# Four batches of a state-space and mixture-of-experts layer on one core: softplus in two groups, routing and scatters at earlier places of the loop, and the products with C shared out anew

## The chip, the cores and the metric

One core of a Trainium2 chip runs the whole layer in one launch. The number that counts is the device time of that launch in microseconds. The five engines (TensorE, VectorE, ScalarE, GpSimd, SyncE for transfers) each run their own list of instructions in order and meet only at semaphores.

## The reference, cut to what matters

x has 4 batches of 512 rows of 512. Three sublayers, each `x = x + f(layernorm(x))`:

```python
# 1 state-space mixer: 1024 channels d, 16 states n, 512 steps t
xz = in_proj @ x ; x, z = split(xz)
x = silu(depthwise_conv4(x)) ; dt, B, C = split(x_proj @ x)
delta = softplus(dt_proj @ dt + bias)            # [512, 1024]
h[t] = h[t-1] * exp(delta * A) + (delta * u) * B[t]   # for each d, n
y[t] = sum_n h[t] * C[t]
out = out_proj @ ((y + u * D) * silu(z))
# 2 an int8-quantised gated MLP, weights of each batch
# 3 mixture of experts: softmax router, top 2 of 16, plus 4 shared experts
```

## The kernel before

All is fp32 except the quantised integers (bf16). The 1024 channels lie as 8 blocks of 128 partitions, time along the free axis (512). The program of every engine is `phase1(b, b-1)` and `scan_stage(b, ...)` for b = 0 to 3, then `phase1(None, 3)` and a last stage without a scan.

**phase1(a, m)** interleaves two batches. For batch a: transposes of the normalised x (`head`), the projections `xi` with the convolution (`conv`, VectorE) and its silu, the small projections `bc_dt`, `dl` (input of the softplus, into bank 4 or 5), `z`, and the softplus. For batch m = a - 1: the last output of the mixer, the residual, and the quantised MLP (`Quant`: reduce, diag, scales, integers, transposed; `linear` on TensorE) in two layers. The order is written out by hand in each engine's phase1.

The softplus is relu(v) + ln(1 + e) - err/(1 + e) with e = exp(-|v|) and err the rounding error of 1 + e. ScalarE did it two blocks at a time: Abs, Exp, ReLU, plus one, Ln, and Exp(-Ln) for the reciprocal (L625 to L651), with a table load wherever the function changes. VectorE made the error term (L848), GpSimd added and subtracted (L484). z stood between the groups. Tiles: `pairs` and `work` serve as scratch; from the scan on they are the ring of products and `dBu`.

**scan_stage** is a loop over p = 0 to 135 on ScalarE, VectorE and TensorE, 128 scan units (block c // 16, state c % 16) and a tail; GpSimd loops over k, one pair of units each. Unit c: ScalarE writes exp(delta * A) into `R[c % 3]`, banks 4 to 6 (L666); GpSimd has made (delta * u) * B for two units, one *chunk* of 128 x 1024 (L521, four slots); VectorE runs the scan in place (L863) and one iteration later the product with C into `prod`, eight slots (L871); GpSimd adds the two products of a pair (L528, at k - 3), TensorE adds the sum into bank 7 by a product with the identity (L1336, at p = 2m + 5), and `gated` (L877, L880) closes each block of 16. From p = 113 TensorE also makes seven output products (`mixer_out`, L1486).

In the stages of b > 0 the experts of batch b - 1 stand between: 8 shared visits (p = 4 to 32, every fourth) and 23 routed ones (from p = 38, every third), each with gate and up products (L1383), tanh, two VectorE instructions and a down product (L1407). The router is cut in pieces on VectorE: `logits` (p = 5), `choice` in 7 steps from p = 10, `places` in 8 steps from p = 20, with `rank` on TensorE at p = 18. GpSimd then scatters the tokens to xs_dram (L541; k = 16 to 19, two transfers each, slot i and row tile t), SyncE reads them back in rows of 128 behind a wait for all scatters (`load_experts`), TensorE transposes them (`row_transposes`, L1367, first at p = 34). Results go to ys_dram, are gathered (L553, k = 60 to 63) and combined (L915, p = 130). The layernorm of the next batch's x runs inside too: statistics at p = 60, normalisation on VectorE (L824) at p = 66.

Of the kernel before, what the change touches and what calls it, by code (L numbers as in the profile page):

```python
# [92 lines left out]

def nsum_at(m):
    return 2 * m + (7 if m % (NS // 2) == 0 else 5)


LINKS = {"A": 1 + 2 * NBLK + NBLK, "LN": 8, "G": 40}
# [4 lines left out]
def build(nc, x, w_in, conv_w, xp_w, dt_w, dt_b, a_log, d_skip, out_w, gu_w, gu_wT, dn_w, dn_wT, gate_w,  # L103
          exp_w, out):
    with ExitStack() as ctx:
# [47 lines left out]
        rstd = sb("rstd", [P, TT])  # L153
        col = sb("col", [P, 9, 4])
# [50 lines left out]
        sp_inv = [late_pairs[:, i, :] for i in range(4)]  # L205
        sp_ln = [work[:, 2048 + i * T:2048 + (i + 1) * T] for i in range(4)]
        sp_w = [work[:, 4096 + i * T:4096 + (i + 1) * T] for i in range(4)]
# [13 lines left out]
        def width(v):  # L221
# [11 lines left out]
            "sp_abs sp_exp relu_ready sp_w_ready sp_ln_ready sp_inv_ready sp_err_ready sum_ready delta_ready "  # L233
            "du_ready dbu_ready da_ready scan_done prod_done pair_ready nsum_done y_done "
# [44 lines left out]
        def _(sp):  # L279
# [29 lines left out]
            def load_gate_up(b):  # L309
# [3 lines left out]
                sp.wait_ge(S["prod_done"], UNITS * b + UNITS - 12)  # L313
                sp.dma_start(guw, gu_w[b]).then_inc(S["xw_in"], 16)

            def load_mlp_down(b):

                sp.wait_ge(S["prod_done"], UNITS * b + UNITS - 4)
# [66 lines left out]
            def load_experts(be):  # L385
# [65 lines left out]
        def _(pool):  # L451
# [32 lines left out]
            def softplus(a, m):  # L484
                pool.wait_ge(S["sp_ln_ready"], NBLK * a + m + 1)
                nc.gpsimd.tensor_tensor(delta[:, m, :], delta[:, m, :], sp_ln[m % 4], ALU.add  # L486
                                        ).then_inc(S["sum_ready"], 1)
                pool.wait_ge(S["sum_ready"], NBLK * a + m + 1)
# [18 lines left out]
            def scan_stage(b, scan, experts):  # L507
# [8 lines left out]
                def chunk(k):  # L516
# [3 lines left out]
                    wait(pool, "scan_done", UNITS * b + 2 * (k - CHUNK_SLOTS + 1))  # L520
                    nc.gpsimd.tensor_tensor(  # L521
# [3 lines left out]
                def pair(m):  # L525
                    lo, hi = prod[2 * (m % PAIR_SLOTS)], prod[2 * (m % PAIR_SLOTS) + 1]
                    pool.wait_ge(S["prod_done"], UNITS * b + 2 * m + 2)
# [58 lines left out]
        def _(sc):  # L586
# [156 lines left out]
            def phase1(a, m):  # L743
                if a is not None:
                    for t in range(TT):
                        head(a, t)
# [873 lines left out]
```

## Time and profile before

| | us |
|---|---|
| median of 3 runs (2019.26 to 2023.7) | 2022.62 |
| the profiled execution | 2020.51 |
| its span | 2018.6 |
| scan stage of batch 0 | about 128 to 374 |
| scan stages of batches 1, 2, 3 | begin at 519, 980, 1441 |
| last stage, experts alone | from about 1822 |

A row of groups gives line, engine, operation, output <- inputs, shapes, count, then busy us, mean ns of one, idle us before them and what ended it. In the timeline a bracket holds the idle time before an instruction and its releaser. "(x16)" in the stage table is a count. One matrix product of fp32 shows as two MATMUL records.

### The profile page before, as it was taken

How to read it: one execution, taken by the hardware profiler on the slowest of the kernel's cores; microseconds unless marked ns; L12 is line 12 of the kernel's file. 1: busy time of each engine (PE TensorE's matmuls, PEld its weight loads, DVE VectorE, ACT ScalarE, POOL GpSimd, SP SyncE). 2: the span in 40 equal slices, each digit the busy share in tenths (PEclk: the TensorE clock that was granted, in tenths of full speed). 3: DMA queues.
4: the chain of work that ended last, by engine and by line, in shares of the span. 5: the costliest groups of instructions: out<-in, count | busy, mean ns of one | idle time of the engine just before them, and what ended most of it. 6: DMA issues, size and time to landing. Idle time of an engine off the chain costs nothing.

```text
span 2018.6 us, 18589 instructions
## 1 busy us (share of the span) xinstructions
PE 1413.2 (70%) x4944; PEld 790.7 (39%) x4952; DVE 1482.2 (73%) x2425; ACT 818.2 (41%) x1344; POOL 1135.8 (56%) x707
## 2 busy tenths in 40 slices
PE   7825546996574788897574777897575878648773
PEld 3301112443443454343442554343343554236562
DVE  3259999686695999686695999696596999673111
ACT  3753333257422454247522445147622554021121
POOL 0279999203867799302866889402767999300101
PEclk9965555997687999998687989998687999767996
DMA  3360000333124663522223664523213663402785
GB/s 99 126 234 0 0 0 5 136 121 110 68 74 144 200 202 127 182 88 97 100 77 130 205 192 140 189 73 114 103 66 120 216 218 125 182 0 79 247 296 171
DMA packets 99016, 255.23 MB, mean 126 GB/s; under 512 B 11488, under 2 KB 11616, under 8 KB 93792
## 3 DMA queue, kind: packets, MB, share of 16 engines
q1 hardware_dynamic: 91680, 233.08, 34.3%
q0 software_dynamic: 5120, 16.78, 2.4%
q10 hardware_dynamic: 2112, 4.19, 0.6%
q8 instruction: 40, 0.66, 0.1%
q14 instruction: 64, 0.52, 0.1%
HBM read 211.02 MB, written 42.99 MB: 126 GB/s over the span
## 4 chain that ended last, share of the span: by engine, by line
POOL 29%; PE 21%; DVE 19%; issue 15%; ACT 11%; DMA 4%; SPq 0%; POOLq 0%; DVEq 0%; ACTq 0%
POOL work L521 16%; DVE bank L863 6%; POOL work L528 5%; PE bank L1383 4%; POOL pairs L528 4%; PE bank L1296 3%; PE bank L1306 3%; DMA ew_up<-in_exp_w 2%; PE bank L1486 2%; DVE u L842 2%; DVE pairs L871 1%; DVE work L871 1%; POOL xs_dram L541 1%; PE bank L1343 1%; POOL du L513 1%
## 5 line engine op out<-in xcount | busy, mean ns | idle before, releaser
L863 DVE TENSOR_TENSOR_SCAN bank<-bank,work 128x512 f32<-128x512 f32 x512 | 624.1, 1220 | 30.2 <-POOL work L521 30.2
L666 ACT ACTIVATE bank<-delta,A_sb 128x512 f32<-128x512 f32 x512 | 353.5, 691 | 641.4 <-DVE pairs L871 325.1
L521 POOL TENSOR_TENSOR work<-du,BB 128x1024 f32<-128x1024 f32 x256 | 604.7, 2364 | 0.8
L1383 PEld LDWEIGHTS bank<-xT,ew_up 128*128 128x128 f32 x1472 | 200.2, 203 | 114.5 <-issue 90.8
L1383 PE MATMUL bank<-xT,ew_up 128*128 128x128 f32 x1472 | 208.8, 288 | 43.7 <-issue 24.0
L1336 PE MATMUL bank<-pairs,ident 128*128 128x512 f32 x256 | 160.8, 734 | 93.2 <-POOL pairs L528 66.7
L528 POOL TENSOR_TENSOR work<-work 128x512 f32<-128x512 f32 x128 | 162.7, 1272 | 62.0 <-DVE work L871 60.9
L1336 PE MATMUL bank<-work,ident 128*128 128x512 f32 x256 | 166.6, 744 | 42.4 <-POOL work L528 42.3
L528 POOL TENSOR_TENSOR pairs<-pairs 128x512 f32<-128x512 f32 x128 | 163.1, 1274 | 54.7 <-DVE pairs L871 53.3
L871 DVE TENSOR_TENSOR pairs<-bank,CB 128x512 f32<-128x512 f32 x256 | 172.2, 673 | 3.0 <-PE bank L1336 3.0
L871 DVE TENSOR_TENSOR work<-bank,CB 128x512 f32<-128x512 f32 x256 | 171.8, 673 | 0.0
L1407 PE MATMUL bank<-ew_dn,etm 128*128 128x512 f32 x184 | 108.3, 672 | 73.4 <-ACT xT L702 73.4
L1306 PE MATMUL bank<-xT,wst 128*128 128x512 f32 x256 | 124.0, 630 | 6.0 <-ACT zg L616 6.0
L1383 PE MATMUL bank<-x3T,ew_up 128*128 128x256 f32 x512 | 125.3, 401 | 0.5 <-DMA ew_up<-in_exp_w 0.5
L486 POOL TENSOR_TENSOR delta<-delta,work 128x512 f32<-128x512 f32 x32 | 52.9, 1652 | 128.2 <-ACT work L647 128.2
L1486 PE MATMUL bank<-wst,zg 128*128 128x512 f32 x256 | 120.1, 616 | 5.8 <-DVE zg L880 4.4
L471 POOL TENSOR_TENSOR col<-col,halfpow 128x4 f32<-128x4 f32 (+1 forms) x8 | 8.2, 1020 | 205.0 <-DVE col L981 205.0
L1296 PE MATMUL bank<-xT,wst 128*128 128x512 f32 x256 | 119.7, 615 | 2.7 <-ACT xT L594 2.7
L1367 PE MATMUL bank<-ident,hm 128*128 128x128 f32 x368 | 60.9, 292 | 81.1 <-DMA hm<-xs_dram 69.2
L887 DVE SCALAR_TENSOR_TENSOR etm<-etm,bank 128x128 f32<-128x128 f32 (+1 forms) x124 | 38.7, 312 | 104.1 <-ACT etm L691 99.3
L1336 PEld LDWEIGHTS bank<-pairs,ident 128*128 128x128 f32 x256 | 51.1, 225 | 162.8 <-POOL pairs L528 65.4
L1383 PEld LDWEIGHTS bank<-x3T,ew_up 128*128 128x128 f32 x512 | 103.1, 203 | 29.3 <-issue 12.9
(174 smaller groups left out, 2038.2 us busy)
## 6 DMA issues: line engine op xcount, KB each, us to landing
ew_up<-in_exp_w SPq DMA_DIRECT2D x124, 512.0 KB, 3.7
ew_dn<-in_exp_w SPq DMA_DIRECT2D x124, 256.0 KB, 4.1
hm<-xs_dram SPq DMA_DIRECT2D x92, 256.0 KB, 4.6
ys_dram<-xT SPq DMA_DIRECT2D x92, 256.0 KB, 4.3
wst<-in_w_in SPq DMA_DIRECT2D x64, 256.0 KB, 2.7
BB<-bc_dram SPq DMA_DIRECT2D x16, 1024.0 KB, 4.9
CB<-bc_dram SPq DMA_DIRECT2D x16, 1024.0 KB, 7.1
wst<-in_out_w SPq DMA_DIRECT2D x32, 256.0 KB, 3.6
```

The costliest lines, as they stand in the source:

```text
L521: nc.gpsimd.tensor_tensor(dBu[:, k % CHUNK_SLOTS, :, :], du[:, j % 2:j % 2 + 1, :].broadcast_to([P, 2, T]), BB[:, n0:n0 + 2, :], ALU.mult) ...
L528: nc.gpsimd.tensor_tensor(lo, lo, hi, ALU.add).then_inc(S["pair_ready"], 1)
L666: nc.scalar.activation(R[q % RING][:, :], delta[:, j, :], ACT.Exp, scale=A_sb[:, j, n:n + 1]).then_inc(S["da_ready"], 1)
L863: V.tensor_tensor_scan(R[q % RING][:, :], R[q % RING][:, :], dBu[:, c // 2 % CHUNK_SLOTS, c % 2, :], 0.0, ALU.mult, ALU.add).then_inc(S["s ...
L871: V.tensor_tensor(prod[c % (2 * PAIR_SLOTS)], R[q % RING][:, :], CB[:, n, :], ALU.mult).then_inc(S["prod_done"], 1)
L1296: ins = mm(ps[:, :], wst[:, slot, k * P:(k + 1) * P], xT[:, k, :], start=(k == 0), stop=(k == KD - 1))
L1306: ins = mm(bank[6 + m % 2][:, :], wst[:, slot, k * P:(k + 1) * P], xT[:, k, :], start=(k == 0), stop=(k == KD - 1))
L1336: mm(Y[:, :], ident[:], prod[2 * (m % PAIR_SLOTS)], start=(m % (NS // 2) == 0), stop=(m % (NS // 2) == NS // 2 - 1)).then_inc(S["nsum_done ...
L1367: ins = nc.tensor.transpose(rows_bank(r)[:, k * P:(k + 1) * P], xs[:, n % 2, k * P:(k + 1) * P], ident[:])
L1383: ins = mm(gu_bank(v)[:, part * n:(part + 1) * n], ew_up[:, q % UP_RING, part * D + k * P:part * D + (k + 1) * P], rhs, start=(k == 0), st ...
L1407: mm(down_ps[1][:, :], eT[:, v % 2, 0:P], ew_dn[:, q % DOWN_RING, :], start=True, stop=True).then_inc(S["down_done"], 1)
L1486: ins = mm(acc[t][:, :], zg[:, k, t * P:(t + 1) * P], wst[:, slot, :], start=(k == 0), stop=(k == NBLK - 1))
```

## The change

Softplus: two groups of four blocks. ScalarE keeps Abs, Exp and Ln; ReLU, plus one, the reciprocal and the last addition go to VectorE; GpSimd subtracts the error term. All z come after it or between its groups, and the scan's first decay waits for them. Routing: pieces at earlier p, two steps an iteration; the scatters at k = 11 and 12, four each, the gathers at 59 and 60. Products: unit c with c % 8 == 7 is scanned straight into `prod` and multiplied by C on GpSimd; pairs of odd m are no longer added by GpSimd, TensorE adds both products. The normalisation of the next x moves to ScalarE (p = 68 to 74), VectorE keeps the shift. The load of x stands behind three loads of rows.

```diff
-ROUTE_EXP_AT = 9
-ROUTE_PROB_AT = 10
-ROUTE_POS_AT = 20
-RANK_AT = 18
-RANK_VISIT = 4
-SCATTER_AT = 16
-GATHER_AT = 60
+ROUTE_EXP_AT = 6
+ROUTE_PROB_AT = 8
+RANK_AT = 14
+RANK_VISIT = 3
+ROUTE_POS_AT = 16
+SCATTER_AT = 11
+GATHER_AT = 59
+def on_pool(c):
+    return c % 8 == 7
+def dve_products(q):
+    return q - q // 8
...
 # SyncE, load_experts
-                if be + 2 < B:
-                    load_x(be + 2)
                 for j in range(ROUTED + 6):
+                    if j == 3 and be + 2 < B:
+                        load_x(be + 2)
...
 # GpSimd, softplus
-                nc.gpsimd.tensor_tensor(delta[:, m, :], delta[:, m, :], sp_ln[m % 4], ALU.add
...
-                nc.gpsimd.tensor_tensor(delta[:, m, :], delta[:, m, :], sp_w[m % 4], ALU.subtract
-                                        ).then_inc(S["delta_ready"], 1)
+                nc.gpsimd.tensor_tensor(delta[:, m, :], delta[:, m, :], sp_e[m % 4], ALU.subtract
+                                        ).then_inc(S["delta_less"], 1)
 # GpSimd, chunk and pair
+                    if k == 2:
+                        pool.wait_ge(S["delta_ready"], NBLK * (b + 1))
...
-                    nc.gpsimd.tensor_tensor(lo, lo, hi, ALU.add).then_inc(S["pair_ready"], 1)
+                    if m % 2 == 0:
+                        pool.wait_ge(S["prod_done"], dve_products(UNITS * b + 2 * m + 2))
+                        nc.gpsimd.tensor_tensor(lo, lo, hi, ALU.add).then_inc(S["pair_ready"], 1)
+                    elif on_pool(2 * m + 1):
+                        pool.wait_ge(S["scan_done"], UNITS * b + 2 * m + 2)
+                        nc.gpsimd.tensor_tensor(hi, hi, CB[:, (2 * m + 1) % NS, :], ALU.mult).then_inc(S["pool_prod"], 1)
 # ScalarE
+            def head_apply(a, t):
+                sc.wait_ge(S["x_in"], 16 * (a + 1))
+                sc.wait_ge(S["a_shift_ready"], a + 1)
+                nc.scalar.activation(xn[:, t, :], xn[:, t, :], ACT.Identity, scale=rstd[:, t:t + 1],
+                                     bias=shift[:, t:t + 1]).then_inc(S["a_xn_ready"], 1)
-            def softplus(a, pair):
-                ms = (2 * pair, 2 * pair + 1)
+            def softplus(a, group):
+                ms = range(4 * group, 4 * group + 4)
...                                                # Relu, Identity and Exp(-Ln) removed
 # VectorE
+            def relu(a, m):
+                ve.wait_ge(S["sp_abs"], NBLK * a + m + 1)
+                V.tensor_scalar(delta[:, m, :], bank[4 + m % 2][:, :], dtb[:, m:m + 1], 0.0, ALU.add, ALU.max
+                                ).then_inc(S["relu_ready"], 1)
+            def one_more(a, m):
...
+                V.tensor_scalar(sp_w[m % 4], sp_e[m % 4], 1.0, None, ALU.add).then_inc(S["sp_w_ready"], 1)
+            def lost(a, m):
...
+                link(V.scalar_tensor_tensor(out=sp_e[i], in0=sp_w[i], scalar=1.0, in1=sp_e[i],
+                                            op0=ALU.subtract, op1=ALU.subtract))
...
+                link(V.reciprocal(du[:, 1, :], sp_w[i]))
+                V.tensor_tensor(sp_e[i], sp_e[i], du[:, 1, :], ALU.mult).then_inc(S["sp_err_ready"], 1)
             def softplus(a, m):
                 ve.wait_ge(S["sp_ln_ready"], NBLK * a + m + 1)
+                ve.wait_ge(S["delta_less"], NBLK * a + m + 1)
+                V.tensor_tensor(delta[:, m, :], delta[:, m, :], sp_ln[m % 4], ALU.add).then_inc(S["delta_ready"], 1)
 # VectorE, order in phase1 (m's steps between): relu 0-3 | q1.reduce, diag, scales |
 #   one_more 0-3, lost 0-3 | q1.integers | softplus 0-3 | q1.transposed | relu 4-7 |
 #   second residual, statistics, norm | one_more 4-7, lost 4-7, softplus 4-7
 # TensorE, nsum
-                    mm(Y[:, :], ident[:], prod[2 * (m % PAIR_SLOTS)], ...)
+                    if m % 2 == 0:            # as before
...
+                    else:
+                        pe.wait_ge(S["prod_done"], dve_products(UNITS * b + 2 * m + 2))
+                        if on_pool(2 * m + 1):
+                            pe.wait_ge(S["pool_prod"], (UNITS * b + 2 * m + 2) // 8)
+                        mm(Y[:, :], ident[:], prod[2 * (m % PAIR_SLOTS)], start=False, stop=False)
+                        mm(Y[:, :], ident[:], prod[2 * (m % PAIR_SLOTS) + 1], start=False,
+                           stop=(m % (NS // 2) == NS // 2 - 1)).then_inc(S["nsum_done"], 1)
 # TensorE, order in phase1: ... bc_dt 6 | integers 0 | bc_dt 7 | linear 0 | dl 0, 1, z 0, dl 2, 3 |
 #   gated_rows | z 1 | diag_rows 1 | z 2 | scale_rows 1, integers 1 | dl 4, 5, z 3, dl 6, 7 | linear 1 | z 4-7
```

## Rows read from the trace of the kernel before

**Rows 1.** The page, engine busy time: us, share of the span, instructions
```profile
PE 1413.2 (70%) x4944; PEld 790.7 (39%) x4952; DVE 1482.2 (73%) x2425; ACT 818.2 (41%) x1344; POOL 1135.8 (56%) x707
```

**Rows 2.** Stage table: stretch, length, busy us (count), granted clock, DMA share, GB/s
```profile
125.00:379.00 254.00, 144.52 (x200) 44.10 (x200) 239.92 (x286) 87.78 (x128) 239.21 (x139) 0.59 0.12 44
379.00:520.00 141.00, 105.64 (x336) 49.63 (x336) 91.84 (x195) 83.80 (x127) 29.55 (x22) 0.87 0.29 105
520.00:840.00 320.00, 233.64 (x903) 146.67 (x904) 281.52 (x411) 119.67 (x210) 254.53 (x152) 0.86 0.45 147
...
720.00:760.00 40.00, 33.29 (x175) 23.06 (x176) 38.99 (x58) 21.65 (x40) 37.67 (x22) 0.96 0.70 222
```

**Rows 3.** Waits: VectorE, TensorE at 521:834; VectorE at 1442:1745 (total, times, longest)
```profile
DVE bank L877 <- PE bank L1336: 21.1, 1, 21.1
...
PE bank L1407 <- ACT xT L702: 24.4, 19, 3.5
...
DVE bank L877 <- PE bank L1336: 17.5, 1, 17.5
```

**Rows 4.** Timeline at 519:636: start, us, engine, line, operation [idle before, releaser]
```profile
519.43 9.26 POOL L521 TENSOR_TENSOR work<-du,BB 128x1024 f32<-128x1024 f32 x4
...
594.05 0.37 DVE L1242 CAST posi<-xT 128x8 uint32<-128x8 f32 x1
...
619.38 0.97 POOL L541 DMA_INDIRECT xs_dram<-xn,posi  x1 [2.34 <-issue]
...
628.41 1.11 PE L1367 MATMUL bank<-ident,hm 128*128 128x128 f32 x4 [22.70 <-DMA hm<-xs_dram]
...
634.35 0.76 DVE L877 SCALAR_TENSOR_TENSOR bank<-u,dsk,bank 128x512 f32<-128x512 f32 x1 [21.11 <-PE bank L1336]
```

**Rows 5.** Timeline, ends of the scan stages of batches 0 and 1
```profile
375.01 1.88 PE L1336 MATMUL bank<-work,ident 128*128 128x512 f32 x4
...
829.25 3.28 DVE L915 SCALAR_TENSOR_TENSOR ew_dn<-ew_dn,tw,x 128x512 f32<-128x512 f32 x3 [7.32 <-DMA ew_up<-ys_dram,posi]
```

**Rows 6.** Timeline, last stage: the places of the tokens, the rows read back
```profile
1863.93 0.17 DVE L1242 CAST posi<-xT 128x8 uint32<-128x8 f32 x1
...
1878.80 0.80 SPq L368 DMA_DIRECT2D hm<-xs_dram  x2
```

**Rows 7.** Groups by line; the last one at 521:834 alone
```profile
L863 DVE TENSOR_TENSOR_SCAN bank<-bank,work 128x512 f32<-128x512 f32 x512 | 624.1, 1220 | 30.2 <-POOL work L521 30.2
L521 POOL TENSOR_TENSOR work<-du,BB 128x1024 f32<-128x1024 f32 x256 | 604.7, 2364 | 0.8
...
L871 DVE TENSOR_TENSOR pairs<-bank,CB 128x512 f32<-128x512 f32 x256 | 172.2, 673 | 3.0 <-PE bank L1336 3.0
...
L528 POOL TENSOR_TENSOR pairs<-pairs 128x512 f32<-128x512 f32 x128 | 163.1, 1274 | 54.7 <-DVE pairs L871 53.3
...
L824 DVE TENSOR_SCALAR xn<-xn,mv,rstd 128x512 f32<-128x512 f32 x4 | 7.4, 1914 | 0.0
```

**Rows 8.** Timeline of batch 0's first phase: normalisation, one z
```profile
10.61 1.92 DVE L824 TENSOR_SCALAR xn<-xn,mv,rstd 128x512 f32<-128x512 f32 x4 [1.17 <-POOL rstd L471]
...
60.77 3.60 PE L1306 MATMUL bank<-xT,wst 128*128 128x512 f32 x8
```

**Rows 9.** Groups by line and shape: reciprocals, alone and second of two
```profile
L990 DVE RECIPROCAL col<-col 128x4 f32<-128x4 f32 x4 | 0.7, 178 | 0.1
...
L990 DVE RECIPROCAL col<-col 128x2 f32<-128x2 f32 x4 | 0.7, 166 | 0.1
...
L1175 DVE RECIPROCAL xT<-xT 128x4 f32<-128x4 f32 x4 | 0.6, 146 | 0.0
L1061 DVE RECIPROCAL col<-col 128x2 f32<-128x2 f32 x4 | 0.5, 134 | 0.0
```

**Rows 10.** Timeline of the phase before batch 1's scan
```profile
472.23 0.29 DVE L1023 TENSOR_SCALAR BB<-BB 128x256 bf16<-128x256 f32 x1 [5.14 <-ACT BB L731]
...
482.81 2.73 DVE L1038 SCALAR_TENSOR_TENSOR BB<-bank,rr,CB 128x512 f32<-128x512 f32 x4 [1.89 <-PE bank L1467]
```

More of the change, by code:

```diff
@@ L723, in scan_stage @@
                                 y_rows(r)
+                    if scan and b + 1 < B:
+                        for t in range(TT):
+                            if p == NORM_AT + 2 + 2 * t:
+                                head_apply(b + 1, t)
             def magic_rows(m, layer, side):
@@ L772, in phase1 @@
                     softplus(a, 0)
-                    z(a, 2)
-                    z(a, 3)
-                    softplus(a, 1)
+                    for i in range(3):
+                        z(a, i)
                 if m is not None:
@@ L780, in phase1 @@
                 if a is not None:
-                    z(a, 4)
-                    z(a, 5)
-                    softplus(a, 2)
-                if a is not None:
-                    z(a, 6)
-                    z(a, 7)
-                    softplus(a, 3)
+                    softplus(a, 1)
+                    for i in range(3, NBLK):
+                        z(a, i)
             for b in range(B):
@@ L923, in scan_stage @@
                         scan_unit(p)
-                    if scan and 1 <= p <= UNITS:
+                    if scan and 1 <= p <= UNITS and not on_pool(p - 1):
                         product(p - 1)
@@ L930, in scan_stage @@
                             logits(b - 1, link)
[L931 to L934 removed]
+                        for step in range(7):
+                            if p == ROUTE_PROB_AT + step // 2:
+                                choice(b - 1, link, step)
+                        for step in range(8):
+                            if p == ROUTE_POS_AT + step // 2:
+                                places(b - 1, link, step)
                         for v in range(VISITS):
@@ L1124, in phase1 @@
                     gated_rows(m)
+                if a is not None:
+                    for i in range(4):
+                        relu(a, i)
+                if m is not None:
                     q1.reduce()
                     q1.diag()
-                if a is not None:
-                    softplus(a, 0)
-                if m is not None:
                     q1.scales()
                 if a is not None:
-                    softplus(a, 1)
+                    for i in range(4):
+                        one_more(a, i)
+                    for i in range(4):
+                        lost(a, i)
                 if m is not None:
@@ L1135, in phase1 @@
                 if a is not None:
-                    softplus(a, 2)
+                    for i in range(4):
+                        softplus(a, i)
                 if m is not None:
@@ L1139, in phase1 @@
                 if a is not None:
-                    softplus(a, 3)
+                    for i in range(4, 8):
+                        relu(a, i)
                 if m is not None:
@@ L1146, in phase1 @@
                 if a is not None:
-                    softplus(a, 4)
-                    softplus(a, 5)
-                if a is not None:
-                    softplus(a, 6)
-                    softplus(a, 7)
+                    for i in range(4, 8):
+                        one_more(a, i)
+                    for i in range(4, 8):
+                        lost(a, i)
+                    for i in range(4, 8):
+                        softplus(a, i)
                     assert linkA[a].n == LINKS["A"], ("A", linkA[a].n)
```

136 lines of the change are left out of this document (65 added, 71 removed).

## The prediction

> **What bounds the kernel now.** I read the page's engine shares first [rows 1]: no engine is busy over 73% of the span, so the answer differs by stage. The table by stage [rows 2] splits it. The scan stage of batch 0 (125 to 379 us) has VectorE at 239.9 and GpSimd at 239.2 us of 254: both full. The scan stage of batch 1 with the experts of batch 0 (520 to 840) has VectorE at 281.5 of 320, GpSimd at 254.5, TensorE at 233.6. The phase between scans (379 to 520) has nobody full: a chain of waits over five engines. Then the waits by stage [rows 3]: in the stages of batches 1 and 2 VectorE stands once for 21.1 us at L877, in batch 3 for 17.5, always behind TensorE; and TensorE itself stands 22.7 us for the rows read back from xs_dram. The timeline [rows 4] tells the story: the places of the tokens are ready on VectorE at 594.05, the eight scatters end with the one at 619.38, the rows reach TensorE at 628.41. TensorE runs its instructions in order, so the sums of products behind that transposition stand still, and VectorE stops when it needs a finished block.
>
> **The routing and scatters sooner.** The places move from iteration 27 of the scan loop to iteration 19, the scatters from k = 16 to 19 to k = 11 and 12 of GpSimd's loop. An iteration costs 2.4 us there: the first chunk is done at 521.8, and VectorE begins its long wait, in iteration 37, at 634.35 - 21.11 = 613.2 [rows 4]. So the places come some 19 us sooner. The scatters then take 8 x 1.27 us plus the 2.34 us that the eighth waits [rows 4], and one chunk of 2.36 between: 15 us; landing and read-back take under 9 more (619.38 to 628.41, with a load of x ahead that now comes later). That is 24 us after iteration 19, and TensorE wants the rows at iteration 34, 14 iterations or 31 us later. The waits of 21.1, 21.1 and 17.5 us go: -59.7. Moved past the queues: on GpSimd four scatters (5.1 us) stand ahead of chunk 12 and four (7.6 us) ahead of chunk 13. VectorE holds four to six scan units ahead, about 9 us, against 17.5 us until chunk 13 is done: about 4 us of new starvation per stage, +12. On SyncE the load of x comes behind three loads of rows; its reader is at iteration 60, so that costs nothing. Gathers at k = 59 and 60 instead of 59+1 to 59+4: at the end of the stage VectorE waited 7.3 us for the last of them [rows 5]; that goes, but TensorE is late next (below), so 3 us: -9 in three stages. In the last stage, without a scan, the places come after one visit less: 1863.93 [rows 6] becomes about 1855.5 (TensorE ranks behind the third visit instead of the fourth, 5 us a visit, and VectorE no longer waits for a fourth and fifth expert). The rows are asked for at 1878.80 now [rows 6] and at 1870.3 then; TensorE's own visits hold it until 1876.7, and it began with the rows 2.6 us after the request, at 1881.4: -4.7 at least, -8.5 at most; I take -6.
>
> **Products.** One of eight products leaves VectorE. Of its 0.67 us [rows 7] 0.08 lie under the next instruction: 0.59, 16 times a stage. Sixteen scan units cost VectorE now 16 x 1.73 + 1.37 = 29.1 us, then 27.8. GpSimd's eight chunks, eight additions and one du cost 8 x 2.36 + 8 x 1.27 + 1.27 = 30.3 us [rows 7]; four additions fewer and two products more (a product taken at the price of an addition) make 27.8. The scan into SBUF instead of PSUM no row shows; I take the same 1.22, with 0.1 us either way, 6 us in all. In batch 0 the bound was GpSimd, 8 x 30.3 = 242.5; with both engines at 27.8 and a little jostling I take 28.2: -17. Behind it TensorE: 32 more sums a stage, each two records, and four records take 1.88 us at full clock with 0.15 of it the end of the last [rows 5]: 0.43 a record, 0.87 a sum. From iteration 113 it is full already, with 7 outputs of eight such records. The five more sums there end 4.3 us later, and that end starts the next phase. Batch 0: -17 + 4.3 = -12.7, say -12. In batches 1 to 3 VectorE is the bound: 16 x 0.59 = 9.4, and the normalisation of the next x, four instructions that take 7.4 us in these stages [rows 7] where four such took 1.92 with GpSimd idle [rows 8], goes to ScalarE (4 x 0.69, which waits for products 1 us at a time anyway): 7.4 less 0.2 for what stays. Together -16.6 in three stages, -49.8.
>
> TensorE in these stages: 320 - 233.6 = 86.4 us free, 27.8 more work and a stage 34 us shorter leave 24. The 24.4 us for ScalarE's copies [rows 3] I read as slack, since ScalarE comes to such a copy only behind the decays that follow VectorE's pace. But it is down to some 5% in the routed part, so I add 5 us a stage: +15.
>
> **The softplus in two groups of four.** What goes: ten of sixteen table loads a phase on ScalarE, the second exponential and one GpSimd addition. What comes, on VectorE, eight times a phase: ReLU 0.67, plus one 0.46 (four of its kind take 1.92, [rows 8]), a subtraction 0.70, a reciprocal, a product 0.62, a sum 0.61. No row shows a reciprocal of 512 elements. Small ones do [rows 9]: in the same place 4 elements take 178 ns and 2 take 166, and as the second of a pair 146 and 134: 12 ns for two elements both times, 6.2 ns each, so 178 + 508 x 6.2 = 3.35 us. From below the bound is 0.68 (the nearest full-size instruction, a reduction or product); from above 4.3 (the same rows with 2 ns of misreading on each side, 8 ns an element). I take 3.35, since two pairs agree. A group's four then take 4 x 4.7 = 18.8 us, and they are on the path.
> The Trainium skill (VectorE: DVE Perf Modes, the 8-slice pipeline) says the reciprocal iterates with a repeat count of 8 where simple operations give one result a cycle. By that rule at its 0.96 GHz (an estimate) it would be 4.27 us; the rows above stand at three quarters of it, and by it the sum would be 30 us longer.
>
> Phase of batch 1, step by step. Without z0 and z1 ahead of it the chain up to the first linear comes 1.5 us sooner, but the transposes of the gated rows wait behind dl2, dl3 and two ReLUs; the scales end near 463.9 instead of 465.8. Then plus one, 1.8, and the four, 18.8: VectorE reaches the integers at 484.5, where it now does at 472.23 [rows 10]. ScalarE, held by its Ln until then and by z2, is ready at 477. The first sums and the transposed integers, 3.8, the ReLUs of the second group behind dl6 and dl7, which stand behind z3: the second residual starts at 494.3 (482.81 now). Its 11.4 us to the end of the normalisation stay: 505.7. Plus one and four more: 526.4, GpSimd's subtraction and du 2.5: the first chunk at 528.9, against 519.43. +9.5 a phase, +28.5 in three. z7, which waits for ScalarE's Ln, ends at 521 and stays hidden. SyncE's weights of the output and the last two broadcasts wait for z4 to z7, until 520.8; they land by 535 and are wanted at 540.
> Phase of batch 0: the start is 4.5 us later, since ScalarE alternates between normalising and copying (four rounds of 2.6 us where VectorE took 1.92 in all and TensorE followed, [rows 8]); without z0 and z1 (3.60 us each, [rows 8]) the projections end 6.4 us sooner. Then 60 us to the first chunk, as now 58.7: -0.5.
>
> **Sum.** -0.5 - 12 + 28.5 - 59.7 + 12 - 9 - 49.8 + 15 - 6 = -81.5. The profiled execution took 2020.51 us (span 2018.6 and 1.9 around it), 0.1% below the median 2022.62. 2020.5 - 81.5 = 1939; 1940 on the scale of the median.
>
> **Rivals.**
> 1. The reciprocal is cheap, 0.7 us (for it: it is one instruction like the others; against: the slope of 12 ns in two pairs). Each group loses 10.6 us; the end is then held by z5 to z7, so the first scan comes 10 us before today's: 20 us less in four phases: 1862.
> 2. It costs 4.3 us: 32 x 0.95 = +30: 1970.
> 3. TensorE's slack is latency, not pace. Then most of the 27.8 us a stage is on the path (for it: TensorE is busy 33.3 of 40 us at 720 to 760, [rows 2]; against: no long wait of VectorE for a sum stands there). +17 in three stages: 1990.
> 4. Slower: TensorE's clock. It is granted 0.59 in batch 0's stage and 0.86 in batch 1's [rows 2], and one sum takes twice as long at the half level (1.2 GHz instead of 2.4). With the new work TensorE is the bound below (233.6 + 27.8) x 0.86 / 286 = 0.79, and the stage is as slow as before below 0.70. At 0.65 a stage takes 346 us, 26 more than now: 2020 - 12 + 28 - 6 + 78 = 2108. Against it: the long stall in which TensorE idles goes, and it has more to do.
>
> **Chances.** Forecast 0.58, rival 1 0.07, rival 2 0.13, rival 3 0.15, rival 4 0.07. The forecast's own spread (stall left over, bursts on GpSimd, scan into SBUF) is 20 us each way. 1906 to 1990 leaves out rivals 1 and 4 and a little more. Within 0.2% is what cannot be told from no change; only a mixture of 3 and 4 lands there, 0.02. Faster 0.91, slower 0.07.
>
> **What will show it.** Right: no wait of VectorE above 5 us at L877's counterpart inside stages 1 to 3; RECIPROCAL 128x512 near 3.35 us, 32 times; GpSimd busy some 20 us less a stage; the phases between scans near 150 us instead of 141; batch 0's scan stage near 242; TensorE above 90% busy in the routed part with a granted clock of 0.95. Wrong: a reciprocal off by 1 us moves the time by 30 us; VectorE idle for sums or chunks by more than 10 us a stage; a routed row still late.

## The result, and the profile after

| | before | after |
|---|---|---|
| median, us | 2019.26 (2014.76 to 2023.70, 5 runs) | 2012.45 (2006.61 to 2013.95, 5 runs) |
| ratio to before | | 0.9947, 95% interval 0.9931 to 0.9963 |
| span of the profiled execution, us | 2018.6 | 2011.6 |

The change gains half a per cent. The forecast was 1940, with 1906 to 1990 as its range, so it was wrong by far more than the measurement's uncertainty. Differences between kernels are given below in us as a difference of ratios times 2020.

The page of the changed kernel, engine busy time and the group of the new reciprocals (line, engine, operation, shapes, count, busy us, mean ns, idle before):

```profile
PE 1493.4 (74%) x5208; PEld 831.6 (41%) x5208; DVE 1595.8 (79%) x2477; ACT 728.3 (36%) x1232; POOL 1010.7 (50%) x611
...
L890 DVE RECIPROCAL du<-work 128x512 f32<-128x512 f32 x32 | 107.3, 3353 | 1.1
```

VectorE is busy for 114 us more than in [rows 1], though products were taken from it: the reciprocals alone are 107. The table of the changed kernel's stages, with the columns of [rows 2]:

```profile
135.00:374.00 239.00, 152.76 (x256) 56.02 (x257) 227.89 (x269) 88.87 (x131) 217.13 (x121) 0.78 0.18 69
374.00:530.00 156.00, 109.28 (x344) 50.34 (x344) 129.59 (x227) 60.46 (x96) 18.54 (x13) 0.86 0.23 80
530.00:832.00 302.00, 251.58 (x960) 153.88 (x961) 271.04 (x394) 119.73 (x212) 234.02 (x137) 0.90 0.50 164
```

The phase between two scans (second row) took 156 us where it took 141, and VectorE (third number) is busy for 130 us of it, where it was for 92. In the scan stage with experts (third row) VectorE has 10 us less to do, GpSimd 20 less, TensorE 18 more. VectorE's waits in that stage (waiter, releaser, us in total, times, longest):

```profile
DVE bank L908 <- POOL work L535: 14.9, 2, 8.5
DVE bank L922 <- PE bank L1398: 7.7, 4, 4.1
DVE pairs L916 <- PE bank L1391: 2.8, 1, 2.8
DVE xT L1214 <- PE bank L1405: 2.0, 1, 2.0
DVE work L908 <- PE bank L1398: 1.6, 1, 1.6
```

The wait of 21.1 us for TensorE [rows 3] is gone. In its place stand two waits for a chunk of GpSimd (14.9 us together) and nine shorter ones; the longest are shown. With the start of VectorE's work in each stage and the end of its last gated block as marks, the two traces divide as follows, in us:

| stretch | forecast | measured |
|---|---|---|
| phase of batch 0, to the first scan | -0.5 | 127.9+2.4 to 135.2+3.1: +8.0 |
| scan stage of batch 0 | -12 | 248.1 to 236.0: -12.1 |
| phases before batches 1 to 3 | +28.5 | 15.5, 13.3 and 14.2 longer: +43.0 |
| scan stages of batches 1 to 3: VectorE's busy time | -49.8 | -13.7, -13.7, -6.6: -34.0 |
| the same: its idle time (-59.7 +12 -9 +15) | -41.7 | 33.8 to 31.0, 33.7 to 31.8, 29.2 to 29.0: -4.9 |
| last stage | -6 | -7.0 |
| sum | -81.5 | -7.0 |

Three rows miss: idle time by 37 us, busy time by 16, the phases between the scans by 15; batch 0's phase adds 8. Below, the length of a phase or stage is taken from one run's trace with these same marks, and it need not sum to the difference of the medians: the profiled execution of a kernel lay up to 8 us from its median.

### The profile page after: what moved, and what is told of

It reads as the page before. It is cut to its first block, busy times and chain, and to the rows that moved or that the text cites. A ratio compares the mean times of both kernels' runs of the same rounds, so it can differ in the third digit from the quotient of the medians.

```text
span 2011.6 us, 19064 instructions
## 1 busy us (share of the span) xinstructions
PE 1493.4 (74%) x5208; PEld 831.6 (41%) x5208; DVE 1595.8 (79%) x2477; ACT 728.3 (36%) x1232; POOL 1010.7 (50%) x611
## 4 chain that ended last, share of the span: by engine, by line
DVE 30%; PE 26%; POOL 19%; issue 17%; DMA 3%; ACT 3%; SPq 1%; DVEq 0%; POOLq 0%; ACTq 0%
POOL work L535 10%; DVE bank L908 7%; DVE du L890 5%; PE bank L1445 4%; PE bank L1548 4%; PE bank L1350 3%; DMA ew_up<-in_exp_w 3%; PE bank L1391 2%; POOL work L543 2%; DVE u L863 2%; PE bank L1379 2%; POOL pairs L543 1%; PE bank L1397 1%; DVE pairs L916 1%; POOL work L546 1%
## 5 line engine op out<-in xcount | busy, mean ns | idle before, releaser
L908 DVE TENSOR_TENSOR_SCAN bank<-bank,work 128x512 f32<-128x512 f32 x448 | 543.1, 1220 | 46.9 <-POOL work L535 46.9
L1360 PE MATMUL bank<-xT,wst 128*128 128x512 f32 x256 | 132.6, 672 | 82.5 <-ACT zg L640 82.5
L502 POOL TENSOR_TENSOR delta<-delta,pairs 128x512 f32<-128x512 f32 x32 | 51.5, 1610 | 234.4 <-DVE pairs L891 234.4
L916 DVE TENSOR_TENSOR work<-bank,CB 128x512 f32<-128x512 f32 x192 | 128.8, 671 | 0.0
L1391 PE MATMUL bank<-work,ident 128*128 128x512 f32 x128 | 78.5, 699 | 61.3 <-POOL work L543 61.3
L1350 PE MATMUL bank<-xT,wst 128*128 128x512 f32 x256 | 116.8, 603 | 2.7 <-ACT xT L611 2.7
L1360 PEld LDWEIGHTS bank<-xT,wst 128*128 128x128 f32 x256 | 54.9, 219 | 154.2 <-ACT zg L640 87.2
L543 POOL TENSOR_TENSOR work<-work 128x512 f32<-128x512 f32 x64 | 81.0, 1266 | 68.6 <-DVE work L916 68.5
L486 POOL TENSOR_TENSOR rstd<-mv,halfpow 128x4 f32<-128x4 f32 x12 | 12.4, 1029 | 199.6 <-DVE mv L833 199.6
L890 DVE RECIPROCAL du<-work 128x512 f32<-128x512 f32 x32 | 107.3, 3353 | 1.1
L1391 PE MATMUL bank<-pairs,ident 128*128 128x512 f32 x128 | 77.1, 688 | 40.5 <-POOL pairs L543 22.0
```

The source lines that it names most:

```text
L543: nc.gpsimd.tensor_tensor(lo, lo, hi, ALU.add).then_inc(S["pair_ready"], 1)
L890: link(V.reciprocal(du[:, 1, :], sp_w[i]))
L908: V.tensor_tensor_scan(prod[c % (2 * PAIR_SLOTS)] if on_pool(c) else R[q % RING][:, :], R[q % RING][:, :], dBu[:, c // 2 % CHUNK_SLOTS, c ...
L916: V.tensor_tensor(prod[c % (2 * PAIR_SLOTS)], R[q % RING][:, :], CB[:, n, :], ALU.mult).then_inc(S["prod_done"], 1)
L1350: ins = mm(ps[:, :], wst[:, slot, k * P:(k + 1) * P], xT[:, k, :], start=(k == 0), stop=(k == KD - 1))
L1360: ins = mm(bank[6 + m % 2][:, :], wst[:, slot, k * P:(k + 1) * P], xT[:, k, :], start=(k == 0), stop=(k == KD - 1))
```

## The experiments

**The four parts, each alone on the kernel before.** The edits are those of the diff shown ahead of the prediction: (1) the softplus with its order of z and linears, (2) the products, (3) routing, scatters and gathers, (4) the normalisation of x on ScalarE.

> The kernel before with the grouped softplus alone (with its new order of z and of the linears on TensorE). Theory (the chain on VectorE): the phases between the scans were 14.8, 12.7 and 13.5 us longer in the changed kernel and the first scan came 0.7 us later behind its chunk, four times; all of that is the softplus, and in the phase of batch 0 0.6 of the 7.3 us: +44 us, about 2063. Rival (the phases grew because TensorE leaves each scan stage late with its extra sums): the softplus alone costs what was forecast, 3 x 9.5 less 6.4 at the start: +22, about 2041.

> The kernel before with the products alone (one in eight on GpSimd, every second pair summed by TensorE). Theory: VectorE is the bound in all four scan stages, and 15 products of 0.59 us leave it: -8.8 +1.7 (TensorE's later end) in batch 0, in batches 1 to 3 only what comes after the stall in iteration 37 counts, -5.9 each: -25 us, about 1994. Rival (TensorE's slack is latency): its 27.8 us a stage come onto the path and the gain is under 12 us, 2007 or more.

> The kernel before with the router, scatters and gathers sooner, in bursts of four, alone. Theory (the stall goes, but the bursts starve VectorE of chunks: 6.5 us at the scatters, 9 at the gathers, the small router operations collide for 2 more): -6 in the stages of batches 1 and 2, -3 in batch 3, -7 in the last: -22, about 1997. Rival (as forecast, starvation only 4 us a stage and the gathers a gain of 3): -63, about 1956, so the loss would lie in an interplay with the other parts.

> The kernel before with the normalisation of the next x on ScalarE alone. Theory (VectorE is the bound in batch 0's stage too): +6.7 at the start, where ScalarE alternates between normalising and copying, -5.0 in batch 0's stage, -6.4 in those of batches 1 and 2: -11, about 2008. Rival (GpSimd is the bound in batch 0's stage, as forecast, and hides it there): -6, about 2013.

| part alone | median, us | ratio to before, 95% interval | difference |
|---|---|---|---|
| softplus | 2067.71 | 1.0249 (1.0225 to 1.0273) | +50 |
| products | 1991.52 | 0.9867 (0.9847 to 0.9886) | -27 |
| routing | 1978.57 | 0.9802 (0.9785 to 0.9820) | -40 |
| normalisation | 2014.46 | 0.9970 (0.9954 to 0.9986) | -6 |

The softplus is a loss of 50 us by itself, a little over what the theory said. The phases of that kernel are 156.2, 157.2 and 158.9 us long, with no product moved, so it is not TensorE's late end that made them grow. The products follow the theory. Routing alone lies between theory and forecast, and the theory fails in two places: the scan stages of batches 1 to 3 are 13.2, 9.5 and 7.0 us shorter, twice what it said, and the last stage gains 14 us instead of 7. The normalisation gains as little as the rival said, but the rival's reason does not hold: its trace has a first chunk at 135.4 instead of 127.9 us and a stretch of eight scans shorter by 5.6 us in batch 0's stage, of which 2.8 come back as a wait near the end. That trace is of the fastest of its eight executions and its span is 11.5 us shorter, as the theory said; the median says 6. The four parts sum to -23; the whole change gave -11 (0.9947).

**Where the parts meet.** Two parts together, and the whole without one part:

> The kernel before with two parts, the sooner routing and the products. Alone they gave -42 and -29 us; all four parts alone sum to -31 and the whole change gave -7. Theory (the missing 24 us lie between these two: once the stall is gone, TensorE with 27.8 us more to do is late by some 8 us a stage, at iterations 37, 88 to 95 and at the end): about 1973. Rival (the two add up, 1949, and the missing part lies with the longer softplus or the normalisation).

> The changed kernel without the softplus part (routing, products and normalisation stay). Theory (the softplus costs in the change what it costs alone, 47 us): 1965. Rival (the 11 us still missing between the parts alone and the whole, after the 13 found between routing and products, come from the softplus: its longer phases bring a cost of their own): 1954.

> The changed kernel without the products part. Alone the products gave 29 us. Theory (13 to 24 us of them are lost to TensorE's lateness once the stall is gone): 2017 to 2028. Rival (they add up): 2041.

| kernel | median, us | ratio, 95% interval |
|---|---|---|
| routing and products | 1965.65 | 0.9716 (0.9688 to 0.9744) |
| all but the softplus | 1953.74 | 0.9667 (0.9642 to 0.9692) |
| all but the products | 2019.77 | 0.9989 (0.9976 to 1.0003) |

The products are worth 27 us alone, 17 on top of the routing (0.9802 to 0.9716) and 8 in the whole change (0.9989 to 0.9947). So the first run lies between theory and rival, and the third where the theory put it. The softplus costs 50 alone and 57 inside (0.9667 to 0.9947): the second run lies on its rival, but the intervals hardly tell 57 from 50. In the traces the four phases cost the same (48 us alone, 47 inside), and the scan stages are 9 us longer with the softplus than without it. Without the products the routing, the softplus and the normalisation just cancel. VectorE's waits in the stage of batch 1 of that kernel without the products, up to the stage's end, show where their gain went:

```profile
DVE bank L883 <- POOL work L520: 18.7, 2, 11.9
DVE bank L897 <- PE bank L1365: 2.5, 1, 2.5
DVE xT L1189 <- PE bank L1372: 2.0, 1, 2.0
DVE pairs L891 <- PE bank L1365: 1.0, 1, 1.0
```

It waits for TensorE 5.5 us; the changed kernel, shown above, waits 14.1 (7.7 + 2.8 + 2.0 + 1.6). In the stages of batches 2 and 3 it waits for TensorE 4.4 and 7.0 us against 13.8 and 12.3: 23 us more in three stages, while its waits for chunks are 6 us shorter. The stages are 299.3, 297.5 and 294.4 us long without the products and 298.8, 299.6 and 293.6 with them. So in the stages with experts the products bring nothing: 6 us less work on VectorE, and 5 to 8 us more waiting. All their remaining gain is batch 0's stage, 244.7 to 236.0. Alone they shortened the other stages by 7 to 8 us each, with the stall of 20 us still there; beside it VectorE waits for TensorE only 6 us in batch 1's stage. That TensorE catches up during the stall is how this is read; no run shows it by itself.

**The eighth indirect transfer.** This is GpSimd's timeline in the changed kernel, scatters and then gathers of one stage (start, us, operation, idle before and its reason):

```profile
590.22 1.23 POOL L559 DMA_INDIRECT xs_dram<-xn,posi  x1 [3.99 <-DVE posi L1296]
...
600.37 0.96 POOL L559 DMA_INDIRECT xs_dram<-xn,posi  x1 [0.30 <-issue]
605.39 0.97 POOL L559 DMA_INDIRECT xs_dram<-xn,posi  x1 [4.06 <-issue]
...
797.73 0.95 POOL L571 DMA_INDIRECT ew_up<-ys_dram,posi  x1 [0.30 <-issue]
804.87 0.94 POOL L571 DMA_INDIRECT ew_up<-ys_dram,posi  x1 [6.18 <-issue]
805.84 2.35 POOL L535 TENSOR_TENSOR work<-du,BB 128x1024 f32<-128x1024 f32 x1
```

And this is VectorE behind the last of these lines:

```profile
808.29 1.23 DVE L908 TENSOR_TENSOR_SCAN bank<-bank,work 128x512 f32<-128x512 f32 x1 [8.51 <-POOL work L535]
```

Within each half of a burst the transfers leave 1.27 us apart, with one chunk between the halves; the eighth stands 4.1 us at the scatters and 6.2 at the gathers. The kernel puts no wait of its own ahead of it. The chunk behind it comes late by as much, and VectorE has used up its chunks.

```
SCATTER_AT = 12                                    # was 11
...
if k == SCATTER_AT + t: scatter(0, t); scatter(1, t)          # twos again
for n in range(2 * TT):                                       # the eighth late
    if k == (GATHER_AT + n // TT if n < 2 * TT - 1 else GATHER_AT + 5): gather(n // TT, n % TT)
```

> The changed kernel with the scatters in twos at k = 12 to 15, the gathers four at k = 59, three at k = 60, and the eighth five iterations later, behind the last chunk. In the trace the eighth indirect DMA of each burst stands 4.1 us (scatters) and 6.2 us (gathers) behind the seventh, and the chunks behind it stand too. Theory (the eighth waits until the seventh has landed; let it come late, and nothing stands): VectorE idle for chunks falls from 6.3 to under 1 us at the scatters and from 10 to about 1 at the gathers, with 2 us given back to TensorE: -13 a stage, -39, about 1973. Rival 1 (the issues themselves starve it): the eighth's wait is not decisive, half of it stays, about 1992. Rival 2 (TensorE is late by then in any case and takes the place of the chunks): under 12 us in all, 2000 or more.

Measured: 1977.82, ratio 0.9794 (0.9772 to 0.9815), 31 us less than the whole change: by the time it lies between theory and rival 1, by the trace it is the theory at the gathers and half of it at the scatters. GpSimd's timeline of this run:

```profile
617.28 0.97 POOL L559 DMA_INDIRECT xs_dram<-xn,posi  x1 [2.34 <-DVE work L909]
...
795.34 0.96 POOL L571 DMA_INDIRECT ew_up<-ys_dram,posi  x1 [0.30 <-issue]
807.11 0.98 POOL L571 DMA_INDIRECT ew_up<-ys_dram,posi  x1 [0.16 <-issue]
```

and VectorE's waits in the stage of batch 1:

```profile
DVE bank L909 <- POOL work L535: 5.1, 2, 2.9
DVE ew_dn L961 <- DMA ew_up<-ys_dram,posi: 3.6, 1, 3.6
DVE pairs L917 <- PE bank L1392: 2.9, 3, 1.5
DVE bank L923 <- PE bank L1399: 2.3, 2, 1.7
```

Issued 11.8 us behind the seventh, the eighth gather stands nowhere. The scatters in twos still have it standing 2.3 us, 3.4 us behind the seventh. The waits for chunks fall from 14.9 to 5.1 us and VectorE's idle time in the stage from 31.0 to 17.1.

What the eighth waits for can be read where a trace tells when each transfer landed. Two gathers of batch 1's stage, first with routing and products, then with all but the products; in each the seventh with its time from issue to landing, then the seventh and the eighth on GpSimd:

```profile
ew_up<-ys_dram,posi POOLq DMA_INDIRECT x1, 3.5
781.05 0.95 POOL L572 DMA_INDIRECT ew_up<-ys_dram,posi  x1 [0.30 <-issue]
785.17 0.94 POOL L572 DMA_INDIRECT ew_up<-ys_dram,posi  x1 [3.16 <-issue]
```

```profile
ew_up<-ys_dram,posi POOLq DMA_INDIRECT x1, 8.4
808.01 0.96 POOL L552 DMA_INDIRECT ew_up<-ys_dram,posi  x1 [0.30 <-issue]
816.94 0.94 POOL L552 DMA_INDIRECT ew_up<-ys_dram,posi  x1 [7.97 <-issue]
```

The eighth leaves 0.58 us after the seventh has landed, both times. Seven of the traces tell the landings, and there it is so in all 41 bursts in which the eighth stood (0.58 to 0.60 us); in the 15 in which the seventh had landed before the eighth's turn it stood 0.16. So the theory's cause holds, and the wait is as long as the seventh's landing is slow.

> The changed kernel with the eighth gather of a burst four iterations later, the scatters left in fours. Theory (8.5 us of VectorE's wait for a chunk at the gathers go, 1 to 2 come back as a wait for the gather behind the scans): -7 a stage, -20, about 1992; the scatters' 6.3 us stay. Rival (TensorE, late at the end of the stage, takes the place): -5 in all.

```
if k == GATHER_AT + i + (4 if i * t == TT - 1 else 0): gather(i, t)
```

Measured: 1987.70, ratio 0.9829 (0.9812 to 0.9845), 24 us less than the whole change, as the theory said and a little more. So 24 of the 31 us lay at the gathers, a place for which the forecast had a gain; 7 at the scatters.

**The reciprocals.**

> The changed kernel with 1/w as exp(-ln w) on ScalarE again, in the same groups of four, so no RECIPROCAL on VectorE (plus one and the subtraction before the scales, the products behind them). Theory (VectorE's chain sets the phases): 13.4 us less in each of eight groups, less a table load and four exponentials (3.5 us) where nothing covers them: -80, about 1932. Rival (z4 to z7 on TensorE, for which the decays wait, then end the phase): the phases end some 10 us before those of the first kernel at best and the late wait eats the rest: -50, about 1962. That the time stays at 2012 would refute that the reciprocals are on the path.

> The changed kernel without the eight reciprocals a phase: the product takes w itself (the correction of the softplus is then another number). Theory: what the 32 x 3.39 = 108 us of VectorE are worth: all of it if nothing else is near, 1904. Rival (the floor of the phase is TensorE's z): about 20 us a phase at most and a stop at the same floor as the version with the inverse on ScalarE, 1935 to 1960.

```
-                link(V.reciprocal(du[:, 1, :], sp_w[i]))                     # VectorE
...
+                    nc.scalar.activation(sp_w[i], sp_ln[i], ACT.Exp, scale=-1.0)   # ScalarE, group of four
```

This cut is of the run with the inverse on ScalarE, which also puts VectorE's plus one and subtraction ahead of the scales. The other run leaves the reciprocal out and has the order of the changed kernel.

| kernel | median, us | ratio, 95% interval | against the change |
|---|---|---|---|
| inverse on ScalarE | 1931.74 | 0.9575 (0.9548 to 0.9601) | -75 |
| no reciprocal | 1933.14 | 0.9586 (0.9533 to 0.9639) | -73 |

To take the reciprocals away altogether brings no more than to give them to ScalarE. That is the rival's floor in the second run (1933, a little under the rival's 1935 to 1960): by the medians 34 of the 107 us were worth nothing, since something else is as late. By the traces it is more. Against the changed kernel the four phases are 58 us shorter in the first run and 57 in the second, so some 50 of the 107 us were worth nothing there. The rest, 29 and 21 us, lies in the scan stages and the last one; part of it is the eighth gather, which in the first run stood 3.0 and 3.2 us in two stages where it stood 6.2 and 7.5 in the changed kernel. The theory's 1932 for the first run is therefore a right number with a part that it did not name. In both, the first scan waits for a decay (7.4 and 3.6 us before batch 1). The run with the inverse on ScalarE, VectorE and then ScalarE (the silu of z and the first decays) before the scan of batch 1:

```profile
508.65 2.35 DVE L913 TENSOR_TENSOR_SCAN bank<-bank,work 128x512 f32<-128x512 f32 x2 [7.37 <-ACT bank L687]
```

```profile
506.01 0.60 ACT L640 ACTIVATE zg<-bank 128x512 f32<-128x512 f32 x1 [2.84 <-PE bank L1373]
506.63 1.28 ACT L687 ACT_TABLE_LOAD   x1
507.93 1.91 ACT L687 ACTIVATE bank<-delta,A_sb 128x512 f32<-128x512 f32 x3
```

The decays wait for z7, and z7 is late because TensorE stood for ScalarE twice in the phase, each time for the silu of a z that ScalarE takes only behind the logarithms of its group:

```profile
455.51 5.88 PE L1373 MATMUL bank<-xT,wst 128*128 128x512 f32 x8 [7.20 <-ACT zg L640]
493.41 12.57 PE L1373 MATMUL bank<-xT,wst 128*128 128x512 f32 x24 [12.54 <-ACT zg L640]
```

**The start.**

> The changed kernel with batch 0's normalisation on VectorE as before (those of the next x stay on ScalarE). Theory: ScalarE alternates between normalising and copying at the start and is done at 22.4 us instead of 15.7; everything to the first scan hangs on it: -6.7, about 2006. Rival (the linears and the softplus of batch 0 wait for something else): no change.

```
-                        if a == 0: head_apply(a, t)        # ScalarE
...
+            norm_apply(0, xn, xn, mv, rstd, ...)           # VectorE
```

Measured: 2002.89, ratio 0.9913 (0.9890 to 0.9936), 7 us less than the change, as the theory said. The first chunk comes at 128.7 us instead of 135.2.

**The corrections together.**

> The changed kernel with three corrections at once: scatters in twos and the eighth gather late, the inverse on ScalarE, batch 0's normalisation on VectorE. Alone they gave 35, 81 and 8-10 us less. Theory (they lie in different stretches and add up, less 5 where the late end of TensorE already ate the gathers' wait): about 1893. Rival (TensorE becomes the bound of the scan stages once the chunks come in time): 1905 or more.

> The combined version, and ScalarE takes z0 and z3 between the absolute values of a group, where the table of the silu is still loaded, instead of behind the group's logarithms. In the version with the inverse on ScalarE TensorE stood 12.5 and 7.2 us a phase for such an activation, and the first scan stood 7.4 us for decays behind z7. Theory (z on TensorE is the floor of the phase): 6 us less in each of four phases, about 1870. Rival (VectorE's chain is as long as TensorE's): 10 less in all.

> As the version with z in between, with the scatters 3, 3 and 1 at k = 12, 13, 14 and the eighth at k = 16 instead of twos. With twos the eighth still stood 2.3 us and VectorE waited 2.9 us for a chunk. Theory: no wait of the eighth, 2 us a stage, -6 against that version. Rival: three in a row starve VectorE of a chunk themselves, no gain or a loss.

```
                     nc.scalar.activation(sp_e[m % 4], ..., ACT.Abs, ...)      # softplus, ScalarE
+                    if m % 4 == 1: z(a, 3 * group)
...
-                            if k == SCATTER_AT + t: scatter(0, t); scatter(1, t)
+                            if k == SCATTER_AT + n // 3 + (2 if n == 2 * TT - 1 else 0): scatter(n // TT, n % TT)
```

| kernel | median, us | ratio, 95% interval |
|---|---|---|
| combined | 1898.77 | 0.9378 (0.9354 to 0.9401) |
| and z0 and z3 between | 1875.88 | 0.9264 (0.9241 to 0.9287) |
| and scatters 3, 3, 1, 1 | 1865.50 | 0.9217 (0.9193 to 0.9240) |

The combination holds: 115 us less than the change (by the ratios) where the three alone sum to 113. The z between take 23 us more off, as the theory said; in the traces the four phases are 9.4, 6.7, 7.4 and 5.0 us shorter, so TensorE's z were on the path. The last step takes 9; its eighth scatter comes 7.1 us behind the seventh and stands nowhere:

```profile
562.38 1.01 POOL L559 DMA_INDIRECT xs_dram<-xn,posi  x1 [0.17 <-issue]
569.47 1.02 POOL L559 DMA_INDIRECT xs_dram<-xn,posi  x1 [0.16 <-issue]
```

The last version beats both kernels: 7.8% faster than the one before. Its stages with experts take 281.4, 279.5 and 276.9 us, its phases 132.5, 131.3 and 131.3, with 5.8, 3.8, 5.5 and 3.9 us from the first chunk to the first scan. Part of the last 9 us may be its last stage alone, which was 263.2 us long in its profile and 268.0 in that of the version before, though their code is the same there.

## Why the prediction was wrong, step by step

**Idle time in the stages with experts (forecast -41.7, measured -4.9): the step that failed.** Three of its terms did. By what VectorE waited for, in three stages: for chunks and gathers +21 us where the forecast had +3 (+12 - 9), for TensorE -28 where it had -45 (-59.7 + 15); small waits add 2.
- "4 us of new starvation per stage" was 6.4, 7.1 and 6.5. The eighth's wait, which [rows 4] show as 2.34 for transfers spread over 22 us, was carried over as it stood; in a burst of four and three it is 4.1 to 4.9.
- "-9" for the gathers had the wrong sign. The eighth's wait was 5.9 us in the kernel before as well, but behind the last chunk, where GpSimd held up nobody. At k = 59 and 60 three chunks stand behind it: 8.5 us of waiting (9.9 and 8.6 in the next two stages). What went (7.3 us in [rows 5]) came back in the scan, and TensorE's late end (4.1 us) on top. The late gather alone gave back 24 us.
- "+15" for TensorE was half of what it cost. Beyond the stall VectorE waited for it 2.9 us a stage in the kernel before, and 14.1, 13.8 and 12.3 now: +31. The products are 23 of these, by the kernel without them. Yet TensorE was busy for only 252 of 302 us, and the forecast's own sign (over 90% busy in the routed part) came true only in places: 36.70 of the 40 us at 720 to 760, 53.04 of 60 before. The forecast argued that 24 us of free time would hold the work. The free time was there, but not where the sums were due: near iteration 37, near 90 and at the end. Rival 3 named this mechanism and priced it at 17 a stage; the products' 8 lie between that and the forecast's 5.

The stall itself went as described (21.1 us to 4.1 at most for one wait), though the places came at 589.7 us, 56 us behind the first scan instead of 72: 16 us sooner, not 19. The 14 iterations to the rows' due time are 34 us at the forecast's own 2.4, not 31, which only adds to its margin.

**Busy time in the same stages (-49.8, measured -34.0).** The price per product was right: eight iterations take 0.6 us less each time, and the products alone take 8.0 us off VectorE's busy time in batch 1's stage (forecast 9.4). The normalisation alone gave 6.7 there (forecast 7.2), but batch 3's stage has no next x to normalise: the forecast counted three stages where the kernel has the edit in those of batches 0, 1 and 2. The earlier routing alone takes 0.9 off. In the whole change it is 13.7 and not the 15.6 of the three, and the small operations of the router, below, are the likely place of the 2 us; no run shows that by itself.

**Batch 0's stage (-12, measured -12.1): a right number for a wrong reason.** The forecast held GpSimd to be the bound there and gave the normalisation nothing. The products alone shortened the scans by 7.1 us and the normalisation alone by 2.6; in the changed kernel, with both, it is 13.8. VectorE was the bound: between the first and the last scan of the kernel before it stood for 0.4 of 237.7 us.

**The phases (+9.5 each, measured +15.5, +13.3, +14.2).** The reciprocal was right: 3353 ns against 3.35, and rivals 1 and 2 fall with it. A little of that is luck: the 12 ns for two elements in [rows 9] are 6.0 ns each, which gives 3.23 us, and even 6.2 gives 3.33; from 4 elements to 512 the measured slope is 6.25. The group of four was right too: 462.43 to 482.63 is 20.2 us for a forecast of 20.6. What was missed is what stands ahead of each group. VectorE's timeline in the phase before batch 1; the gated block before it ended 4.1 us sooner than in the kernel before, so 4.1 is to be added to compare with the prediction's times:

```profile
449.63 1.61 DVE L872 TENSOR_SCALAR delta<-bank,dtb 128x512 f32<-128x512 f32 x2 [3.32 <-ACT pairs L656]
...
462.43 1.43 DVE L880 TENSOR_SCALAR work<-pairs 128x512 f32<-128x512 f32 x4
...
482.63 1.98 DVE L1070 TENSOR_SCALAR BB<-BB 128x256 bf16<-128x256 f32 x4
...
493.61 1.61 DVE L872 TENSOR_SCALAR delta<-bank,dtb 128x512 f32<-128x512 f32 x2 [3.27 <-ACT pairs L656]
495.13 2.72 DVE L1085 SCALAR_TENSOR_TENSOR BB<-bank,rr,CB 128x512 f32<-128x512 f32 x4
...
526.60 6.77 DVE L897 TENSOR_TENSOR delta<-delta,work 128x512 f32<-128x512 f32 x4
533.29 2.33 DVE L908 TENSOR_TENSOR_SCAN bank<-bank,work 128x512 f32<-128x512 f32 x2
```

The first group starts at 466.5 on the old scale (463.9 forecast), behind ReLUs that wait 3.3 us for dl2 and dl3; the second residual at 499.2 (494.3), behind another such wait and four sums (L897) that were left out there. Together 5 us. The last four sums take 6.77 us instead of 2.4, beside GpSimd's subtraction, du and chunk, and the scan stands behind them: 0.7 more. The softplus alone cost 50 us; the forecast's own steps for it gave 28.5 in three phases and, in batch 0's, -6.4 for the z and +1.3 for 60 us instead of 58.7: 23.

**The start (-0.5, measured +8.0).** The alternation between normalising and copying was seen and priced at 4.5; it is 6.7 (ScalarE's last copy ends at 22.4 us instead of 15.7; 1.28 of it is a table load, done at 0.80 us before and now at 10.95, behind the shift), and the 6.4 us that z0 and z1 gave back were spent by the softplus of the first batch, which took 7 us longer to the first chunk.

**The last stage (-6, measured -7.0)** and **rival 4** (the clock): the granted clock rose instead, from 0.59 to 0.78 in batch 0's stage and from 0.86 to 0.90 in batch 1's, with more work on TensorE. The places came 12 us sooner after the last gated block, the end 7; of the chain that ended last, from 1740 us on, waits for the experts' weights are 20.6% now where they were 17.1%. In the thirteen traces with the sooner routing this stage is between 260.7 and 268.8 us long, also where its code is the same, and in the four without it between 271.7 and 274.9. Why it varies is left open.

## What to carry to other kernels

When a stall is removed, ask what else it had covered: the products were worth 27 us with the stall and 8 in the whole change without it. Average free time of an engine is no cover; ask at each due time how far it is behind. And before issues are bunched on a queue, find the longest wait among them, what ends it and what stands behind it: a wait that costs nothing at the end of a stage costs all of itself three chunks earlier.

## What the runs showed of the hardware

- The eighth of each eight indirect transfers from GpSimd waits until the seventh has landed, and leaves 0.58 to 0.60 us later (41 bursts of seven traces). In all traces it stood 2.3 to 6.6 us at the scatters and 3.0 to 8.0 at the gathers. Put 7.1 us (scatters) or 11.8 (gathers) behind the seventh, it did not stand. Every burst here has eight, so no run shows whether the eighth counts or the last.
- A reciprocal of 512 float32 elements a partition takes 3352 to 3354 ns on VectorE, 32 times of 32 in the changed kernel; against 178 ns for 4 elements [rows 9] that is 6.25 ns an element. The Trainium skill (VectorE: DVE Perf Modes, Walkthrough: the 8-slice pipeline in each mode) speaks of a repeat count of 8. As an estimate from it, at the page's 0.96 GHz, it would be 4.27 us; the measurement decides for three quarters of it.
- Some small operations of VectorE in SBUF end only with the GpSimd instruction that they fall beside. The same cast and the same sum of 16 elements, before and then after:

```profile
555.55 0.68 DVE L1189 CAST xT<-xT 128x8 f32<-128x8 uint32 x1
...
574.72 0.17 DVE L1215 TENSOR_TENSOR xT<-xT 128x16 f32<-128x16 f32 x1
```

```profile
560.32 2.28 DVE L1243 CAST xT<-xT 128x8 f32<-128x8 uint32 x1
...
577.68 2.27 DVE L1269 TENSOR_TENSOR xT<-xT 128x16 f32<-128x16 f32 x1
```

And GpSimd beside the last two:

```profile
560.22 2.35 POOL L535 TENSOR_TENSOR work<-du,BB 128x1024 f32<-128x1024 f32 x1
577.58 2.34 POOL L535 TENSOR_TENSOR work<-du,BB 128x1024 f32<-128x1024 f32 x1
```

Both long ones start 0.10 us behind a chunk and end with it; in the last stage, where GpSimd has no chunk, both take 0.17. This agrees with the Trainium skill (SBUF — State Buffer, SBUF: two separate sides), by which the two engines share a pair of ports that one of them holds for a whole instruction. The page says so of VectorE's instructions with two inputs in SBUF, beside a GpSimd instruction that reads SBUF, and of those in a 2-port mode; whether the cast is in such a mode no trace shows.
- A scan that writes SBUF took 1.21 us (1212 ns, 16 of them in batch 1's stage), one that writes PSUM 1.22 (1221 ns).
